# Biases of q, k, v and LN1's weight and bias folded into q/k/v weights built on the chip, from block 3 on

## The reference

```
xh   = normalise(x)                                  # outer LN, no weights
xn   = normalise(xh) * ln1_w + ln1_b
q, k, v = xn@wq + bq, xn@wk + bk, xn@wv + bv         # 16 heads of 16, fq = elu(q)+1, fk = elu(k)+1
s[h,g]  = sum_d fq[h,d] fk[g,d]                      # per token: 16 x 16 scores between the heads
attn[h] = sum_g s[h,g] v[g] / (sum_g s[h,g] + 1e-6)
y = xh + attn@wo + bo;  a = y + gelu(LN2(y)@fc_w + fc_b)@proj_w + proj_b;  x1 = x + a
z = normalise(x1);  out = x1 + shared(z) + sum over the top 2 of 8 experts of weight * expert(z)
```

## Time and profile before

| | |
|---|---|
| median of 3 runs | 1744.97 us (1744.45 to 1745.19) |
| the profiled execution: its own time | 1744.85 us |
| its span, first to last instruction | 1742.7 us |
| TensorE matmul busy | 1680.7 us (96%) |
| VectorE busy | 1166.9 us (67%) |
| GpSimd busy | 1166.9 us (67%) |
| ScalarE busy | 904.1 us (52%) |
| share of the chain that ended last | PE 89%, ACT 5%, DVE 2%, issue 2% |
| mean granted TensorE clock | 0.985 of full |

### The profile page before, as it was taken

The page is one execution under the profiler, slowest core; times in us unless marked ns, Lnnn a source line. Parts: engine busy times, 40 slices in busy tenths (PEclk is TensorE's granted clock), DMA queues, the critical chain, the costliest instruction groups (busy, mean ns, idle before and its releaser), DMA issues.

```text
span 1742.7 us, 25628 instructions
## 1 busy us (share of the span) xinstructions
PE 1680.7 (96%) x7243; PEld 1227.5 (70%) x7289; DVE 1166.9 (67%) x1968; ACT 904.1 (52%) x2240; POOL 1166.9 (67%) x624
## 2 busy tenths in 40 slices
PE   6899999999999999999999998989999999999997
PEld 4555666666666666666666665578888888888886
DVE  7989999999999999999999993322222222222221
ACT  4356667667667667667667646522322322332322
POOL 5769889889889889889889881413333343343343
PEclk9898999999999999999999999999999999999999
DMA  4302211211211211111111111367777777777764
GB/s 151 116 13 61 62 49 37 62 49 36 61 49 36 61 49 36 59 50 36 54 55 37 37 49 37 92 169 162 165 154 160 165 157 156 167 158 156 168 158 78
DMA packets 89455, 157.20 MB, mean 90 GB/s; under 512 B 8896, under 2 KB 72128, under 8 KB 89024
## 3 DMA queue, kind: packets, MB, share of 16 engines
q1 hardware_dynamic: 60512, 112.58, 20.9%
q0 software_dynamic: 28896, 44.06, 14.9%
HBM read 101.79 MB, written 48.56 MB: 86 GB/s over the span
## 4 chain that ended last, share of the span: by engine, by line
PE 89%; ACT 5%; DVE 2%; issue 2%; DMA 1%; POOL 1%; SPq 1%; POOLq 0%; ACTq 0%; DVEq 0%
PE p_b L1494 17%; PE p_b L1548 13%; PE p_b L1698 10%; PE p_b L1709 10%; PE p_b L1641 8%; PE p_q L1698 7%; PE p_q L1466 6%; PE p_v L1698 4%; PE p_v L1466 3%; PE p_b L1480 2%; PE p_xT L1685 2%; PE p_xT L1626 2%; ACT rows L706 1%; ACT xmid L706 1%; PE p_b L1588 1%
## 5 line engine op out<-in xcount | busy, mean ns | idle before, releaser
L654 POOL DMA_INDIRECT out_rows<-prod_pool,prod x142 | 221.4, 1559 | 387.9 <-ACT prod_pool L949 357.5
L523 POOL TENSOR_TENSOR prod_pool<-prod_pool 128x2048 f32<-128x2048 f32 (+1 forms) x180 | 347.9, 1933 | 14.1
L1548 PE MATMUL p_b<-bT,fc_sb 128*128 128x512 f32 x512 | 231.5, 606 | 1.3 <-ACT bT L865 1.3
L1494 PE MATMUL p_b<-proj_sb,hid 128*128 128x256 f32 x1024 | 230.5, 379 | 0.0
L1494 PEld LDWEIGHTS p_b<-proj_sb,hid 128*128 128x128 f32 x1024 | 189.6, 190 | 29.4 <-issue 0.5
L1026 DVE TENSOR_TENSOR prod<-p_q,eqk 128x4096 f32<-128x4096 f32 (+1 forms) x47 | 184.0, 3914 | 5.3 <-DVE attn L1076 1.0
L1698 PE MATMUL p_b<-prod,exp_up 128*128 128x256 f32 x840 | 187.1, 379 | 0.0
L1063 DVE TENSOR_REDUCE qkv<-prod 128x256 f32<-128x4096 f32 (+1 forms) x47 | 183.7, 3910 | 1.6
L1050 DVE TENSOR_TENSOR prod<-p_q,v_dve 128x2048 f32<-128x2048 f32 (+2 forms) x60 | 177.4, 2956 | 1.5
L574 POOL DMA_INDIRECT rows_sorted<-rows,slot x128 | 125.7, 982 | 78.5 <-issue 34.5
L1035 DVE TENSOR_REDUCE p_q<-prod 128x128 f32<-128x2048 f32 (+2 forms) x60 | 177.4, 2957 | 1.1
(11 more groups left out here) (208 smaller groups left out, 2988.6 us busy)
## 6 DMA issues: line engine op xcount, KB each, us to landing
exp_up<-in_experts SPq DMA_DIRECT2D x71, 768.0 KB
prod<-rows_sorted SPq DMA_DIRECT2D x71, 260.0 KB
xin<-in_x SPq DMA_DIRECT2D x16, 512.0 KB, 3.4
xres<-in_x SPq DMA_DIRECT2D x16, 512.0 KB
xres<-xmid POOLq DMA_DIRECT2D x16, 512.0 KB, 4.6
out_rows<-x SPq DMA_DIRECT2D x16, 512.0 KB, 2.9
exp_dn<-in_experts SPq DMA_DIRECT2D x8, 384.0 KB, 5.8
out_rows<-prod_pool,prod POOLq DMA_INDIRECT x142, 3.8
```

The source lines that it names most:

```text
L523: done(g.tensor_tensor(prod_pool[:, at:at + n * w], prod_pool[:, at:at + n * w], prod_pool[:, at + n * w:at + 2 * n * w], ALU.add))
L654: pool.indirect_dma_start(out=out[:, :], out_offset=bass.IndirectOffsetOnAxis(ap=tok_i[j][:, a:a + 1], axis=0), in_=yg[j][:, a * D:(a + 1) ...
L1494: ins = t_.matmul(o, src[:, k, t * P:(t + 1) * P], w[:, k, :], start=k == 0, stop=bias_at is None and k == chunks - 1)
L1548: ins = t_.matmul(bnk[:], fc_sb[:, k, f * P:(f + 1) * P], bT[:, k, :], start=k == 0, stop=k == KC - 1)
```

## The change

From tile 12 on (block 3 and later; `FOLDED = 3`) the q/k/v projection uses another weight buffer, `wfold`. Since a normalised token sums to zero over its 256 values, `(xhat + 1) @ (ln1_w*W + r/256)`, with the same row r in every row of the matrix, equals `xhat @ (ln1_w*W) + sum(ln1_w*W) + r`. With `r = sum((ln1_b - ln1_w)*W) + bias` this is q, k or v with the bias in it. So for those tiles ScalarE only adds 1 to the transposed tile, in one instruction, and TensorE issues no bias matmuls. Tiles 0 to 11 are computed as before.

The weights are made once: ScalarE computes `ln1_b - ln1_w`, `ln1_w*W` and a matrix `fold_w` with `ln1_b - ln1_w` in every column (body 0); TensorE computes r in all 128 rows, with the bias rows, into two free banks (body 1); VectorE adds r/256 to `wfold` (body 1). Cut to its core:

```diff
+        def folded(n):
+            return not isinstance(n, int) or n >= 4 * FOLDED
 # ScalarE, take_x
-                for k in range(KC):
-                    ins = a.activation(xnT[u % 2][:, k, :], p_xT[:, k * P:(k + 1) * P], ACT.Identity,
-                                       bias=ln_sb[:, 1, k:k + 1], scale=ln_sb[:, 0, k:k + 1])
+                if folded(n):
+                    ins = a.activation(xnT[u % 2][:].rearrange("p k t -> p (k t)"), p_xT[:, 0:D], ACT.Identity,
+                                       bias=one_1[:, 0:1])
+                else: ...
 # ScalarE, body 0, ahead of take_qkv(1, 1)
+            def fold_parts():
+                for k in range(KC):
+                    a.activation(fold_d[:, k:k + 1], ln_sb[:, 0, k:k + 1], ACT.Identity, scale=-1.0,
+                                 bias=ln_sb[:, 1, k:k + 1]).then_inc(fold_diff, 1)
+                    a.activation(wfold[:, k, :], wqkv_sb[:, k, :], ACT.Copy, scale=ln_sb[:, 0, k:k + 1]
+                                 ).then_inc(fold_in, 1)
+                act.wait_ge(fold_diff, KC)
+                for k in range(KC):
+                    a.activation(fold_w[:, k, :], ident[:], ACT.Identity, scale=0.0, bias=fold_d[:, k:k + 1]
+                                 ).then_inc(fold_in, 1)
 # VectorE, body 1, after products_2(1, 1)
+            def fold():
+                dve.wait_ge(fold_psum, 1)
+                dve.wait_ge(fold_in, 2 * KC)
+                for k in range(KC):
+                    for bnk, lo, hi in ((p_b0, 0, 512), (p_b1, 512, 768)):
+                        ins = v.scalar_tensor_tensor(wfold[:, k, lo:hi], bnk[:, 0:hi - lo], 1.0 / D,
+                                                     wfold[:, k, lo:hi], ALU.mult, ALU.add)
...
 # TensorE, project_x
+                    w = wfold if folded(n) else wqkv_sb
...
-                            t_.matmul(bnk[:, 0:hi - lo], xnT[u % 2][:, k, :], wqkv_sb[:, k, lo:hi],
-                                      start=k == 0, stop=False)
+                            ins = t_.matmul(bnk[:, 0:hi - lo], xnT[u % 2][:, k, :], w[:, k, lo:hi],
+                                            start=k == 0, stop=folded(n) and k == KC - 1)
+                    if not folded(n):   # the two bias matmuls stand under this now
...
 # TensorE, body 1, after P(1, 2)
+            def fold():
+                pe.wait_ge(fold_in, 2 * KC)
+                wait(pe, attnT_ready, KC)
+                for bnk, lo, hi in ((p_b0, 0, 512), (p_b1, 512, 768)):
+                    for k in range(KC):
+                        t_.matmul(bnk[:, 0:hi - lo], fold_w[:, k, :], wqkv_sb[:, k, lo:hi], start=k == 0, stop=False)
+                    ins = t_.matmul(bnk[:, 0:hi - lo], bias_rows_bf[:], bias_bf[:, lo:hi], start=False, stop=True)
+                ins.then_inc(fold_psum, 1)
 # TensorE, body 1, ahead of proj (which writes the same two banks)
+                        pe.wait_ge(fold_ready, 1)
 # VectorE, at the start
+            done(v.memset(one_1[:], 1.0))
```

More of the change, by code:

```diff
@@ L60 @@
 POOL_HEADS = 6
+FOLDED = 3
 RANKS_AT = 5
@@ L84, in build @@
         wqkv_sb = sb("wqkv_sb", [P, KC, 3 * D])
+        wfold = sb("wfold", [P, KC, 3 * D])
+        one_1 = sb("one_1", [P, 1])
+        fold_d = sb("fold_d", [P, KC])
         wo_sb = sb("wo_sb", [P, KC, D])
@@ L257, in build @@
         qkv_taken = sem("qkv_taken")
+        fold_diff = sem("fold_diff")
+        fold_in = sem("fold_in")
+        fold_psum = sem("fold_psum")
+        fold_ready = sem("fold_ready")
         feat_ready = sem("feat_ready")
@@ L895, in body @@
                         ln3_finish(c, k)
+                if first:
+                    fold_parts()
                 if more:
@@ L1136, in first_block @@
                 dve.sem_inc(pq_free, 1)
+            def fold():
[3 more added lines that the diff above has]
+                    for bnk, lo, hi in ((p_b0, 0, 512), (p_b1, 512, 768)):
+                        ins = v.scalar_tensor_tensor(wfold[:, k, lo:hi], bnk[:, 0:hi - lo], 1.0 / D, wfold[:, k, lo:hi],
+                                                     ALU.mult, ALU.add)
+                        if k < KC - 1 or lo == 0:
+                            done.later(ins)
+                done.sync()
+                announce(dve, ins, fold_ready, 1)
             def residual_1(c):
@@ L1242, in body @@
                     products_2(c, 1, False)
+                if isinstance(c, int) and c == 1:
+                    fold()
                 if stage_c:
@@ L1463, in project_x @@
                     parts = ((p_qk[u % 2], 0, 512), (p_v, 512, 768))
+                    w = wfold if folded(n) else wqkv_sb
                     for bnk, lo, hi in parts:
                         for k in range(KC):
-                            t_.matmul(bnk[:, 0:hi - lo], xnT[u % 2][:, k, :], wqkv_sb[:, k, lo:hi],
-                                      start=k == 0, stop=False)
[L1468 to L1472, removed]
-                    ins.then_inc(qkv_psum, 1)
+                            ins = t_.matmul(bnk[:, 0:hi - lo], xnT[u % 2][:, k, :], w[:, k, lo:hi],
+                                            start=k == 0, stop=folded(n) and k == KC - 1)
+                    if not folded(n):
+                        if isinstance(n, int) and n == 0:
+                            pe.wait_ge(bias_ready, 1)
+                        for bnk, lo, hi in parts:
+                            ins = t_.matmul(bnk[:, 0:hi - lo], bias_rows_bf[:], bias_bf[:, lo:hi],
+                                            start=False, stop=True)
+                    ins.then_inc(qkv_psum, 1)
+            def fold():
+                pe.wait_ge(fold_in, 2 * KC)
+                wait(pe, attnT_ready, KC)
+                for bnk, lo, hi in ((p_b0, 0, 512), (p_b1, 512, 768)):
+                    for k in range(KC):
+                        t_.matmul(bnk[:, 0:hi - lo], fold_w[:, k, :], wqkv_sb[:, k, lo:hi], start=k == 0, stop=False)
+                    ins = t_.matmul(bnk[:, 0:hi - lo], bias_rows_bf[:], bias_bf[:, lo:hi], start=False, stop=True)
+                ins.then_inc(fold_psum, 1)
             def transpose_block(src, banks, ready, tile_ready=None):
```

4 lines of the change are left out of this document (added).

## The result

The changed kernel takes 1749.91 us in the median of 15 runs (1746.11 to 1752.09), the kernel before 1745.60 in 15 runs (1740.02 to 1747.71). The ratio is 1.0023, 95% interval 1.0016 to 1.0031: about 4 us slower, small but clear. The profiled executions are 1749.91 (span 1747.8) and 1744.85 (span 1742.7).

What follows compares the result with a forecast made beforehand. TensorE was taken to set the pace, in a ring with VectorE close behind. A gain of 6.35 us and clock falls costing 8.85 gave +2.5 on 1744.85, 1747.35; the median 0.12 above: 1747.5, range 1740.5 to 1752.

Steps and rivals of the forecast that it cites:

- the prediction's own line of 1748.5: Upper end of 1741.5 to 1748.5, the 0.2% (3.5 us) band counted as the same time; above it counts as slower.
- Bias matmuls: Between projections on TensorE: a pair costs 0.32 us, 1.28 a block, but only 0.45 a block gained; 6.35 us in all.
- the ring: VectorE and TensorE together bound the block: P(c+1,1) waits for VectorE's L1050, slack 0.13 us, so blocks become 65.42.
- `take_x`: ScalarE's copy of the transposed tile in one instruction: 0.40 us less, so TensorE ends `logits` sooner; bounds 0 to 0.45.
- The pause at `down`: Right behind `logits`, TensorE waits 0.9 us for GpSimd's product (0.5 without ScalarE's gain); in time alone this is free.
- the 0.33 in hand at P(c+1,1): P(c+1,1) reached at 49.47 while VectorE lets it go at 49.80, so 0.33 us of a clock fall is absorbed.
- The clock: Falls at the pause behind `logits`, 2.1 us each, 1.77 after what is in hand; 5 times (4 to 6): 8.85 us.
- at most every other body: After a fall GpSimd is early and the next body has no pause, so at most 6 falls in 13 bodies.
- Building the weights: Before the loop's steady blocks: TensorE 2.9 us, VectorE 2.0, both hidden in waits; `fc` in body 1 still slow; cost 0.
- the end of the stage: P(15,3) with what follows it: a gain of some 0.3 us.
- "GpSimd next": Rival: the clock holds and GpSimd becomes the bound, a gain of 3.0 us, 1742.0; chance 0.20.
- The whole 16.6 us: Rival: all TensorE time of the 52 removed bias pairs is gained, 1728.3; needs slack of 1.3 us; chance 0.02.

Runs made afterwards that it cites:

- the relieved VectorE: Changed kernel, GpSimd's shared product earlier, GpSimd's first halving cut to one eighth, VectorE's products of tile (c,3) leaving out 4 of 16 heads: 1729.87 us, ratio 0.9913.
- The kernel with two copies: Changed kernel with ScalarE's copy of the transposed tile in two instructions of 128 x 128 again: 1749.23 us, ratio 1.0023.
- the kernel before with the three moves: Kernel before, with GpSimd's shared product earlier, VectorE's product ahead of the second residual add, a third of the shared product on VectorE: 1741.38 us, ratio 0.9990.
- its copy with the early product: Kernel before with only GpSimd's shared product moved behind the first halving of the scores instead of the last: 1741.69 us, ratio 0.9996.
- the early product: Changed kernel with GpSimd's shared product moved behind the first halving of the scores instead of the last: 1740.27 against 1743.14 us, ratio 0.9984.
- the last kernel: Changed kernel, GpSimd's shared product earlier, VectorE's product first in bodies 1 to 14, 256 of 1536 shared-product columns on VectorE: 1740.51 us, ratio 0.9970.
- the kernel with a third moved: Changed kernel, GpSimd's shared product earlier, VectorE's product ahead of the second residual add, 512 of 1536 shared-product columns on VectorE: 1737.79 us, ratio 0.9971.
- The two kernels with GpSimd relieved: Changed kernel, GpSimd's shared product earlier, its first halving cut to one eighth: 1742.81 us, ratio 0.9986; the second also omits 4 heads of VectorE's products: 1729.87, 0.9913.

## Why the prediction was right

It forecast 1747.5 in a range of 1740.5 to 1752.0; 1749.91 was measured. The mechanism came as forecast: a small gain per block, a new pause behind `logits`, and a clock that falls there and takes back more than the gain. The size did not come as well: +2.5 us were forecast, the medians are 4.3 apart, and by the prediction's own line of 1748.5 this is the "slower" to which it gave 0.30. By its own steps:

- *Bias matmuls.* 0.45 us a block expected, 0.38 measured: 0.12 ahead of P(c+1,1) (49.81 after L1188 instead of 49.93) and 0.26 behind it instead of 0.32. That the rest of the 1.28 is held by the ring, not lost on TensorE, was argued from a slack of 0.13 and is shown by the relieved VectorE (64.42).
- *`take_x`.* 0.33 instead of 0.40: one instruction takes 0.48 (0.81 for two before), and the transposes of `rows` are 0.34 shorter.
- *The pause at `down`.* Forecast 0.9, found 0.41 to 0.74, 0.57 in the mean, as the profile counts idle time. Counted as the forecast did it is 0.15 more, 0.72: in an unhindered block `down` starts 1.70 us behind the start of `logits`, so at 471.00 + 1.70 = 472.70, and it started at 473.56. Place, releaser and cause were as said, and so was the 0.33 in hand at P(c+1,1) (a wait of 0.36).
- *The clock.* Five falls expected, five found. The five was taken between 4 and 6 and not derived, so that it is exact is luck. So was, in part, the step to it: at the three places in the trace before where the clock fell beside `logits`, TensorE had also stood still for longer (2.16 us at 143.92, 1.16 at 1059.19 and at 1112.00), so that trace did not show half a microsecond to be enough; the changed kernel does. A fall costs TensorE 1.7 us in `down` (2.1 expected; 1.0 in the first, at 275) and the block 1.45 to 1.68 instead of 1.77; the sum is 7.9 instead of 8.85. One argument for "at most every other body" was wrong: the pause does not vanish behind a fall (0.53 at 540.51, after the fall at 474), because GpSimd starts from VectorE's features and moves with them. The kernel with two copies had falls in neighbouring bodies.
- *Building the weights.* As worked out on TensorE and VectorE. TensorE fills the front of its wait and keeps 2.22 of 5.13 us, the four instructions of VectorE take 1.94, its later wait shrinks from 2.65 to 1.71, and `fc` starts in the low clock all the same:

```profile
80.70 2.17 PE L1539 MATMUL p_b<-ident,hid 128*128 128x128 f32 x8 [2.22 <-ACT hid L723]
83.53 16.41 PE L1609 MATMUL p_b<-bT,fc_sb 128*128 128x512 f32 x32 [0.66 <-ACT bT L894]
```

  The row that the prediction wanted unmoved, VectorE's add at 119.92, stands at 120.49. Of these 0.57 us 0.48 are there at the first add of body 1 (74.31 against 73.83), before VectorE and TensorE do their part; that add lies anywhere from 72.82 to 74.61 in the fourteen traces, so the shift can't be put down to the building.
- *The term that was missing.* Between the two profiled executions lie 5.1 us where 2.5 were forecast. Up to body 15 the errors come to 0.9: the gain is 4.9 (0.34 and 12 × 0.38) instead of 6.05, the five blocks with a fall are 8.3 longer and not 8.85, and 0.3 is small lengthenings. The rest, 1.7, is the end of the stage, for which the sum had a gain of 0.3 and the trace has a loss of 1.4. In body 16 TensorE stood still for 2.55 us ahead of the transposes of `attn`, and the clock was low in `wo`, 1054 to 1061.5, and again in `down` from 1068; before, it stood still there for 2.48 us, the clock held through `wo`, and fell once, 1060.5 to 1067.5. That put the add of body 16 2.25 us further behind (1063.20 against 1057.30), of which `down` gave 1.7 back; then the first expert tile waited 1.83 longer for its rows, behind DMAs. The fall in `wo` is nothing that the fold brings alone: eleven of the fourteen traces have it, the kernel before with the three moves among them, and the kernel before, its copy with the early product and the one with two copies have not. What decides it stays open.
- *Of the rivals,* "GpSimd next" gave 3.0 us of gain if the clock held; with the early product it held, and the gain was 2.9 (1743.14 - 1740.27). The number came out by luck, the reason did not hold: GpSimd does run slower than the ring (its L550 starts are 65.67 apart, VectorE's adds 65.57), but nobody waits for it, since with the early product it has 4.0 us in hand at `down` in body 3 and 2.8 still in body 15, and relieving it changed nothing. In the profiled executions of the two kernels with the early product the changed one is 4.7 us ahead at the add of body 15 (988.66 against 993.32); the fall in `wo` of body 16 takes 2.25 of it. The whole 16.6 us was rightly given next to nothing.

## What to carry to other kernels

When TensorE work is removed, ask where TensorE will then stand still and what runs beside that place: half a microsecond behind thin matmuls cost more here than the 0.4 us a block that were gained, while 1.0 to 1.4 us among full ones did not bring the clock down. The remedy was not to remove the wait by adding speed but to move one 3.4 us instruction of the engine waited for ahead of work that nobody was waiting for. And the idle time of an engine is not all that it has in hand: count also how long before its use each of its outputs is done (0.3 us at `down` before, 4.4 with the early product).

## What the runs showed of the hardware

*VectorE behind GpSimd.* In the last kernel VectorE multiplies 128 × 256 of two SBUF tensors while GpSimd multiplies the rest of the same two. Timeline of VectorE, then of GpSimd:

```profile
595.43 0.97 DVE L1286 TENSOR_TENSOR sg_g<-sg_g,sg_u 128x256 f32<-128x256 f32 x1
596.33 1.27 DVE L1194 TENSOR_TENSOR xmid<-xmid,p_b 128x512 f32<-128x512 f32 x2
```

```profile
593.20 2.93 POOL L598 TENSOR_TENSOR sg_g<-sg_g,sg_u 128x1280 f32<-128x1280 f32 x1 [0.16 <-POOL prod_pool L538]
```

GpSimd's instruction ends at 596.13, VectorE's at 596.40, 0.27 later. In the 14 bodies in which GpSimd's instruction was already under way VectorE ends 0.27 to 0.29 after it, whenever it started, and takes 0.97 to 1.32 us; in the last one, where VectorE came first, it took 0.43. With 512 columns, in the kernel with a third moved, it ends 0.54 to 0.56 after GpSimd's in 13 bodies, and in the two bodies where it came before GpSimd's instruction it took 0.69. So it does not run slower beside GpSimd; it waits for the end of the instruction and then does its work. The smaller share on VectorE left GpSimd's instruction longer (2.9 us instead of 2.4) and thus cost more. The Trainium skill ("SBUF — State Buffer", "Who interferes with whom") says this: an instruction of VectorE with two SBUF inputs and one of GpSimd that reads SBUF share a read interface, and the second to issue blocks until the first is done. The traces agree: the distance from GpSimd's end to VectorE's varies by 0.02 us only, while VectorE's own length varies by 0.35.

*The clock.* The Trainium skill ("TensorE: Matmul & The Clock Gate", "Why this matters for your kernels") warns of long idle gaps; by that the clock would have held. Here the granted clock fell to 0.50 behind gaps of 0.35 to 0.74 us where `logits` stood ahead of them, and the measurement decides. Longer gaps elsewhere did not settle it either: in body 16 it held behind 2.48 us in the kernel before and fell behind 2.55 in the changed one. The Trainium skill says elsewhere on that page ("A second HAM failure mode: psum-queue depth-cycling") that frequent short idling between groups of matmuls can make the clock go back and forth. That is nearer to what these traces show, though there the idling comes at every group and here the wait is one in a block of 65 us. What decides in which bodies it falls no run here settled.

*Scatter.* Runs of one kernel on one chip differ by up to 10.5 us. The two kernels with GpSimd relieved show what may be one source. In the profiled execution of the first, VectorE's second residual add of body 2 stood still for something that the profile calls remote; the operand `xres` is written by a DMA. Then P(3,1) ran at a granted clock of 0.50 behind a wait of 2.17 us:

```profile
186.88 0.69 DVE L1207 TENSOR_TENSOR x<-xres,p_b 128x512 f32<-128x512 f32 x1 [2.29 <-remote]
```

```profile
189.91 3.61 PE L1518 MATMUL p_q<-wfold,xnT 128*128 128x512 f32 x4 [2.17 <-DVE prod L1085]
```

The block took 69.33 us instead of 65.27 in the run with the early product. That execution, 1747.41, was the slowest of twelve of its kernel (from 1740.76). The second kernel's execution has the same (a wait of 3.36, a block of 69.31), but at 1730.82 it is only 1 us above its median; of the other twelve traces one has such a wait, 1.20 us. That late transfers make the scatter is thus not shown.
